# Another order for the last two token tiles, a shorter root, half-size own scores, and identity transposes in seven waits of PE

## What is computed

```python
x = x + _L0_xattn_ref(_layernorm(x), ctx_1024, ctx_1024, mask, gamma, beta)   # 64 queries on 1601 rows of context
x = x + _L0_attn_ref(_layernorm(x), W_qkv, W_out)                            # 64 tokens of a batch on each other
x = x + _L0_ffn_ref(_layernorm(x), router_w, expert_w1, expert_w2)           # top 2 of 8 experts, 512 -> 2048 -> 512

# in _L0_ffn_ref
scores = xf @ router_w.T
top_v, top_i = jax.lax.top_k(scores, 2)
routing_w = jax.nn.softmax(top_v, axis=-1)
for e in range(8):
    w_e = jnp.sum(jnp.where(top_i == e, routing_w, 0.0), axis=-1)
    h = jax.nn.gelu(xf @ expert_w1[e].T, approximate=False)
    out = out + h @ expert_w2[e].T * w_e[:, None]
```

## Time and profile before

| | us |
|---|---|
| median of 3 runs | 802.03 (801.93 to 803.76) |
| the profiled execution | 801.91, of it 800.3 between its first and its last instruction |
| PE busy | 740.5 of 800.3 |
| DVE, ACT, POOL busy | 447.5, 304.8, 148.5 |
| streaming stage, full turns (r = 3 to 7) | about 37 each |
| first expert chunk begins on PE | 382.36 |

### The profile page before, as it was taken

The page is one execution under the profiler, slowest core; times in us unless marked ns, Lnnn a source line. Parts: engine busy times, 40 slices in busy tenths (PEclk is TensorE's granted clock), DMA queues, the critical chain, the costliest instruction groups (busy, mean ns, idle before and its releaser), DMA issues.

```text
span 800.3 us, 12058 instructions
## 1 busy us (share of the span) xinstructions
PE 740.5 (93%) x4626; PEld 552.3 (69%) x4626; DVE 447.5 (56%) x1052; ACT 304.8 (38%) x508; POOL 148.5 (19%) x160
## 2 busy tenths in 40 slices
PE   5999899999999999862999899999999999999992
PEld 3453345364545453442999899999999998888882
DVE  4153467676868646755456544555556655566520
ACT  2031112122221211221555354556565565656620
POOL 2133030412213010104201021111210212120201
PEclk9999999999999999985899999999999999999997
DMA  9999999999999999211254455564755757674402
GB/s 340 401 421 383 421 384 384 418 379 423 381 421 367 421 412 400 120 52 35 88 163 183 119 176 186 141 208 161 209 189 170 208 205 205 215 235 167 122 1 27
DMA packets 35133, 198.85 MB, mean 248 GB/s; under 512 B 4540, under 2 KB 4924, under 8 KB 14080
## 3 DMA queue, kind: packets, MB, share of 16 engines
q1 hardware_dynamic: 29680, 187.81, 61.8%
q0 software_dynamic: 4672, 9.11, 6.1%
q10 hardware_dynamic: 720, 1.10, 0.4%
HBM read 188.16 MB, written 9.85 MB: 247 GB/s over the span
## 4 chain that ended last, share of the span: by engine, by line
PE 77%; DVE 8%; DMA 7%; issue 3%; SPq 2%; ACT 1%; POOL 1%; POOLq 0%; DVEq 0%; ACTq 0%
PE ps L756 8%; PE ps L985 8%; PE ps L797 8%; PE ps L987 8%; PE ps L986 8%; PE ps L1007 4%; PE ps L1008 4%; PE ps L1009 4%; PE ps L1014 4%; PE ps L1015 4%; PE ps L1016 4%; DMA arena<-in_w_out 3%; DMA arena<-in_ctx_turned 3%; PE ps L812 3%; PE ps L827 3%
## 5 line engine op out<-in xcount | busy, mean ns | idle before, releaser
L459 POOL TENSOR_TENSOR small<-small 128x1 f32<-128x1 f32 x64 | 20.9, 327 | 618.3 <-DVE yb_space L1510 198.0
L987 PE MATMUL ps<-xT,low_a 128*128 128x288 f32 (+5 forms) x384 | 111.1, 289 | 0.0
L1482 DVE TENSOR_TENSOR h_ring<-hid,h_ring 128x288 fp32r<-128x288 f32 (+5 forms) x128 | 55.6, 435 | 96.4 <-ACT h_ring L1173 93.4
L1168 ACT ACTIVATE hid<-ps 128x288 f32<-128x288 f32 (+5 forms) x128 | 50.6, 395 | 151.2 <-PE ps L987 148.7
L797 PE MATMUL ps<-arena 128*64 128x512 f32 (+1 forms) x416 | 94.5, 598 | 3.0 <-DMA arena<-in_ctx 1.8
L1371 DVE TENSOR_TENSOR low_a<-w_raw_a,high_b 128x2048 fp32r<-128x2048 f32 x32 | 73.2, 2291 | 37.7 <-ACT high_b L1108 36.4
L1061 ACT COPY arena<-ps 128x512 f32<-128x512 f32 (+2 forms) x93 | 43.8, 528 | 122.9 <-PE ps L731 66.7
L756 PE MATMUL ps<-arena 128*64 128x512 f32 x384 | 85.5, 596 | 0.9 <-DMA arena<-in_ctx_turned 0.7
L985 PE MATMUL ps<-xT,high_b 128*128 128x288 f32 (+5 forms) x256 | 74.9, 292 | 0.0
L987 PEld LDWEIGHTS ps<-xT,low_a 128*128 128x128 f32 x384 | 73.5, 191 | 0.0
L986 PE MATMUL ps<-xT,high_b 128*128 128x288 f32 (+5 forms) x256 | 73.4, 287 | 0.0
(11 more groups left out here) (192 smaller groups left out, 1615.7 us busy)
## 6 DMA issues: line engine op xcount, KB each, us to landing
arena<-in_ctx_turned SPq DMA_DIRECT2D x48, 1024.0 KB, 23.3
arena<-in_ctx SPq DMA_DIRECT2D x48, 1024.0 KB, 22.7
w_raw_a<-in_w SPq DMA_DIRECT2D x48, 1024.0 KB, 5.0
w_raw_b<-in_w SPq DMA_DIRECT2D x16, 1024.0 KB, 4.9
arena<-in_mask SPq DMA_DIRECT2D x8, 800.5 KB, 26.8
arena<-in_w_qkv SPq DMA_DIRECT2D x3, 1024.0 KB, 9.4
arena<-in_ctx SPq DMA_DIRECT2D x16, 130.0 KB
out<-res SPq DMA_DIRECT2D x8, 256.0 KB, 22.1
```

The costliest lines, as they stand in the source:

```text
L987: mm = pe.matmul(o, w_low[2 * f][:, cols], high[:, k, 0:w.width], start=False, stop=(k == KC - 1))
L1168: nc.scalar.activation(hid[:, c % 2, 0:w.width], bank(c % UP_BANKS)[:, 0:w.width], ACT.Gelu).then_inc(gelu_done, 1)
L1482: dve.tensor_tensor(h_ring[:, c % RING, 1, 0:w.width], hid[:, c % 2, 0:w.width], h_ring[:, c % RING, 0, 0:w.width].bitcast(F32), ALU.subtr ...
```

## The change

1. **The root** has 7 instructions in place of 9: the guess starts from another constant, a cubic step follows and one Newton step ends it. In `attended` the reciprocal of the row sum moves ahead of the wait for PE.
2. **`own_scores`** multiplies only the two diagonal blocks of 64 x 64 that are used, as 8 matmuls of 64 columns in place of 4 of 128.
3. **`route_first`** forms the difference of the two best scores earlier and signals it with a new semaphore, `ratio_set`, on which ACT's `gate_exp` waits in place of `picked`.
4. **`gates`** is new: five instructions of `route_second` (the token numbers and the two gates) become a function that is called ahead of it. `route_second` keeps four.
5. **The drain** has another order on PE, ACT and DVE, with `fill_order` to match.
6. **`keep_busy(n)`** on PE transposes the identity matrix n times into bank 0, and nobody reads that. It stands at seven places: 6, 16, 12 and 72 times in the drain, and 4 times behind each of the three `turn_x` of window 0.
7. **`gate`** of the last window's first piece waits for a new semaphore, `first_tile_done`, which PE sets at the last matmul of that piece.

```diff
-                    ("u", LAST), ("xr", LAST - 1), ("pt", LAST), ("logit", LAST - 1), ("out", LAST),
-                    ("rank", LAST - 1), ("xr", LAST), ("logit", LAST), ("rank", LAST)):
+                    ("u", LAST), ("pt", LAST), ("xr", LAST - 1), ("out", LAST), ("logit", LAST - 1),
+                    ("xr", LAST), ("logit", LAST), ("rank", LAST - 1), ("rank", LAST)):
...
+                pool.wait_ge(gates_ready, t + 1)
                 pool.wait_ge(pos_ready, t + 1)
...
             def own_scores(t):
                 wait_copied(pe, "g", t)
                 o = open_fill("s", t)
                 for k in range(KC):
-                    mm = pe.matmul(o[:, 0:P], gT[:, k, :], xnT[:, k, :], start=(k == 0), stop=(k == KC - 1))
+                    for b in range(2):
+                        q = slice(64 * b, 64 * b + 64)
+                        mm = pe.matmul(o[q, q], gT[:, k, q], xnT[:, k, q], start=(k == 0), stop=(k == KC - 1))
                 mm.then_inc(filled, 1)
...
+            def keep_busy(n):
+
+                for _ in range(n):
+                    pe.transpose(bank(0)[:, 0:P], ident, ident)
...
             turn_own_probs(LAST - 1)
+            keep_busy(6)
             turn_first(LAST)
             weigh(LAST - 1)
             keys(LAST)
             own_scores(LAST)
             values(LAST)
+            turn_own_probs(LAST)
             turn_second(LAST - 1)
-            turn_own_probs(LAST)
+            weigh(LAST)
             router(LAST - 1)
-            weigh(LAST)
-            ranks(LAST - 1)
+            keep_busy(16)
             turn_second(LAST)
             router(LAST)
+            ranks(LAST - 1)
+            keep_busy(12)
             ranks(LAST)
...
             pe.matmul(bank(6)[:, 0:EXPERTS], ones, cum[TILES], start=True, stop=True).then_inc(count_done, 1)
+
+            keep_busy(72)
...
+                        if final and w.kind == EXPERTS - 1 and t == 0:
+                            mm.then_inc(first_tile_done, 1)
...
                 turn_x(STATIC[0], t)
+                keep_busy(4)
...
             def gate_exp(t):
 
-                act.wait_ge(picked, t + 1)
+                act.wait_ge(ratio_set, t + 1)
...
             copy_probs(LAST)
-            copy_fill("xn", LAST - 1, xnT, shown=by_chunk)
             gate_exp(LAST - 2)
             for j in range(2):
                 split_high(STATIC[0], j)
+            copy_fill("xn", LAST - 1, xnT, shown=by_chunk)
...
             copy_fill("xr", LAST - 1, xrT, shown=by_chunk)
-            split_high(STATIC[0], 2)
+            for j in range(2, 4):
+                split_high(STATIC[0], j)
+            copy_fill("xr", LAST, xrT, shown=by_chunk)
             gate_exp(LAST - 1)
-            copy_fill("xr", LAST, xrT, shown=by_chunk)
-            split_high(STATIC[0], 3)
             gate_exp(LAST)
...
+            def rsqrt(variance):
+
+                own.then_next(dve.tensor_scalar(var, variance, EPS, ROOT_SCALE, ALU.add, ALU.mult))
+                own.then_next(dve.tensor_scalar(rstd.bitcast(I32), var.bitcast(I32), -0.5, GUESS, ALU.mult, ALU.add))
+                own.then_next(dve.scalar_tensor_tensor(out=half, in0=rstd, scalar=rstd, in1=var,
                                                        op0=ALU.mult, op1=ALU.mult))
-                own.then_next(dve.scalar_tensor_tensor(out=rstd, in0=half, scalar=1.5, in1=rstd,
+                own.then_next(dve.scalar_tensor_tensor(out=half, in0=half, scalar=-10.0 / 3.0, in1=half,
+                                                       op0=ALU.add, op1=ALU.mult))
+                own.then_next(dve.scalar_tensor_tensor(out=rstd, in0=half, scalar=5.0, in1=rstd,
+                                                       op0=ALU.add, op1=ALU.mult))
+                own.then_next(dve.scalar_tensor_tensor(out=half, in0=rstd, scalar=rstd, in1=var,
+                                                       op0=ALU.mult, op1=ALU.mult))
+                own.then_next(dve.scalar_tensor_tensor(out=rstd, in0=half, scalar=-64.0 / 3.0, in1=rstd,
                                                        op0=ALU.add, op1=ALU.mult))
...
             def attended(j):
 
+                dve.wait_ge(exp_done, j + 1)
+                own.then_next(dve.reciprocal(inv, rowsum[:, j % 2:j % 2 + 1]))
                 dve.wait_ge(pv_block, j * NBLK + NBLK)
                 moments(bank(NBLK - 1))
-                own.then_next(dve.reciprocal(inv, rowsum[:, j % 2:j % 2 + 1]))
...
+                    if n == 1:
+                        dve.tensor_tensor(ratio[par], best[:, 1:2], best[:, 0:1], ALU.subtract).then_inc(ratio_set, 1)
...
+            def gates(t):
 
                 par = t % 2
                 dve.wait_ge(places_free, t + 1)
+                own.then_next(dve.tensor_copy(meta_i[par][:, :, 1], token.to_broadcast([P, TOP_K])))
+                own.then_next(dve.tensor_scalar(token, token, float(P), None, ALU.add))
+                dve.wait_ge(ratio_ready, t + 1)
+                own.then_next(dve.tensor_scalar(low, ratio[par], 1.0, None, ALU.add))
+                own.then_next(dve.reciprocal(meta[par][:, 0, 0:1], low))
+                dve.tensor_tensor(meta[par][:, 1, 0:1], ratio[par], meta[par][:, 0, 0:1], ALU.mult).then_inc(gates_ready, 1)
...
             route_first(LAST - 2)
             for j in range(2):
                 split_low(STATIC[0], j)
+            gates(LAST - 2)
             route_second(LAST - 2)
...
             copy_pt(LAST)
+            second_norm(LAST)
             route_first(LAST - 1)
-            second_norm(LAST)
+            route_first(LAST)
+            gates(LAST - 1)
             route_second(LAST - 1)
-            route_first(LAST)
+            gates(LAST)
             route_second(LAST)
...
-                    dve.wait_ge(down_done, w.at(PER_CHUNK, FC))
+                    if w.kind == EXPERTS - 1 and t == 0:
+                        dve.wait_ge(first_tile_done, 1)
+                    else:
+                        dve.wait_ge(down_done, w.at(PER_CHUNK, FC))
```

More of the change, by code:

```diff
@@ L50 @@
 HUGE = 3.0e38
-GUESS = float(0x5F3759DF)
-NEWTON = 3
+GUESS = float(0x5F3759DF - 2 ** 31)
+ROOT_SCALE = (1024.0 / 27.0) ** 2
 C_ID, C_TRI, C_ONE, C_ME, C_SPARE, C_EXP = 0, P, 2 * P, 3 * P, 3 * P + 1, 3 * P + 2
@@ L408, in build @@
         xn2_ready = sem("xn2_ready")
-        picked, ratio_ready = sem("picked"), sem("ratio_ready")
+        picked, ratio_set, ratio_ready = sem("picked"), sem("ratio_set"), sem("ratio_ready")
+        gates_ready = sem("gates_ready")
         pos_ready = sem("pos_ready")
@@ L425, in build @@
         h_high_ready, h_ready = sem("h_high_ready"), sem("h_ready")
-        down_done = sem("down_done")
+        down_done, first_tile_done = sem("down_done"), sem("first_tile_done")
         yT_by_act, yT_by_dve = sem("yT_by_act"), sem("yT_by_dve")
@@ L1220, in _ @@
             own = Steps(dve, v_own)
-            def rsqrt_start(v, variance):
-                own.then_next(dve.tensor_scalar(v, variance, EPS, None, ALU.add))
-                own.then_next(dve.tensor_scalar(rstd.bitcast(I32), v.bitcast(I32), -0.5, GUESS, ALU.mult, ALU.add))
-                own.then_next(dve.tensor_scalar(v, v, -0.5, None, ALU.mult))
-            def rsqrt_step(v):
-                own.then_next(dve.scalar_tensor_tensor(out=half, in0=rstd, scalar=rstd, in1=v,
-                                                       op0=ALU.mult, op1=ALU.mult))
-                own.then_next(dve.scalar_tensor_tensor(out=rstd, in0=half, scalar=1.5, in1=rstd,
+            def rsqrt(variance):
+                own.then_next(dve.tensor_scalar(var, variance, EPS, ROOT_SCALE, ALU.add, ALU.mult))
+                own.then_next(dve.tensor_scalar(rstd.bitcast(I32), var.bitcast(I32), -0.5, GUESS, ALU.mult, ALU.add))
+                own.then_next(dve.scalar_tensor_tensor(out=half, in0=rstd, scalar=rstd, in1=var,
+                                                       op0=ALU.mult, op1=ALU.mult))
+                own.then_next(dve.scalar_tensor_tensor(out=half, in0=half, scalar=-10.0 / 3.0, in1=half,
[5 more added lines that the diff above has]
+                own.then_next(dve.scalar_tensor_tensor(out=rstd, in0=half, scalar=-64.0 / 3.0, in1=rstd,
                                                        op0=ALU.add, op1=ALU.mult))
@@ L1244, in normalize @@
                 moments(src)
-                rsqrt_start(var, mv[:, 1:2])
-                for _ in range(NEWTON):
-                    rsqrt_step(var)
+                rsqrt(mv[:, 1:2])
                 return dve.tensor_scalar(dst, src, mv[:, 0:1], rstd, ALU.subtract, ALU.mult)
@@ L1278, in attended @@
             def attended(j):
+                dve.wait_ge(exp_done, j + 1)
+                own.then_next(dve.reciprocal(inv, rowsum[:, j % 2:j % 2 + 1]))
                 dve.wait_ge(pv_block, j * NBLK + NBLK)
                 moments(bank(NBLK - 1))
-                own.then_next(dve.reciprocal(inv, rowsum[:, j % 2:j % 2 + 1]))
```

(14 more changed lines are left out.)

4 lines of the change are left out of this document (2 added, 2 removed).

## The result

The changed kernel takes 795.99 us (median of 4 runs, 794.73 to 796.58) against 801.98 before: a ratio of 0.992, 95% interval 0.9905 to 0.9935. That is 6.0 us less. The forecast was 792.4 with a range from 788.5 to 797.5, so the direction was right and the time lies in the range, but 3.6 us of the expected gain of 9.5 are missing. Where rows of two kernels are compared, part of a difference can be this.

A forecast was written before the change was run, and what follows sets the result against it. PE and full transfers were taken to bound the stream, one chain the drain, PE the expert stage. Stream 1.8, sending 5.4, clock and turning 1.6, end 0.7 sum to 9.5: 801.9 to 792.4 us, range 788.5 to 797.5.

The forecast's parts named there:

- stream, to `turn_own_probs` of tile 5: Streaming stage: shorter own_scores on PE, limited by waits for ACT while POOL holds DVE's cast; 1.8 us gained.
- from there to the norm of tile 7: Drain: shorter roots, own_scores, earlier gate_exp and the new order bring tile 7's norm 6.9 us earlier.
- places of tile 6, less the stream's: Drain, DVE: both route_first, gates and route_second follow the norm, so tile 6's places come only 1.4 us earlier.
- first transfer of send(7), less the stream's: Drain, POOL: the 3.92 us wait for DVE vanishes, POOL's own chain replaces it; tile 7 sent 5.4 us earlier.
- clock in the expert stage: First expert chunks: transposes may keep PE's fast clock; bounds 0 and 2.7 us, middle 1.3 taken.
- end: Last window: DVE gets the first piece before the last piece's matmuls end, so POOL starts 0.7 us earlier.
- at most 0.5 us earlier: Stream, turn 6: POOL's mask instruction cannot start before its mask lands, at most 0.5 us earlier than before.
- from there its own pace counts: Drain: once tile 6's places are sent, POOL needs 4.0 us until it is free for tile 7.
- Casts not held and clock held: First rival: POOL does not hold DVE's casts, stream gives 3.3, clock 2.7; 12.4 us gained, 789.5; chance 0.19.
- transposes don't lift the clock: Second rival, drain: transposes leave PE at 1.2 GHz; 3.0 us gained, 798.9; chance 0.13.
- they are serialised: Slower rival, drain: each of the 72 transposes waits for the one before, 30 us in all; 814; chance 0.03.
- The change doesn't move the chain: Rival, drain: POOL or its transfers stay late, landings 2 us slower, 4 of 9.5 gone; 796.4; within forecast's range.

The follow-up runs named there:

- e7: The changed kernel without the portion of 72 transposes, the six other portions kept; 795.22 us.
- e1: The changed kernel, with DVE starting split_low of blocks 2 and 3 only after POOL's addition in front of send(7); 795.33 us.
- e3: As e1, and tile 6 is finished on DVE before route_first of tile 7, with fill_order to match; 790.2 us.
- e6: The changed kernel, with DVE starting split_low of blocks 2 and 3 only after POOL has issued both transfers of send(7); 793.99 us.
- e8: The changed kernel with tile 6 finished on DVE before route_first of tile 7, without the additional wait ahead of the splits; 791.55 us.
- e10: As e8, without the portion of 72 transposes; 791.57 us.
- e11: As e8, without the portions of 4 transposes behind turn_x; 791.27 us.
- e2: The changed kernel without any identity transposes (keep_busy called nowhere); 798.46 us.
- e9: The changed kernel with only the portions of 4 transposes behind turn_x, without those of 6, 16, 12 and 72; 796.18 us.
- e4: The kernel before with the half-size own_scores and the short root alone; 796.68 us.
- e5: The kernel before with the half-size own_scores alone, the root keeping its 9 instructions; 800.05 us.
- e12: The kernel before with the short root alone; 798.97 us.

## Why the prediction was right or wrong

| step, gain in us | forecast | in the profiled execution |
|---|---|---|
| stream, to `turn_own_probs` of tile 5 | 1.8 | 3.0 (300.53 to 297.54) |
| from there to the norm of tile 7 | 6.9 | 6.4 (353.77 to 344.38, less 3.0) |
| places of tile 6, less the stream's | 1.4 | 1.4 (359.70 to 355.26, less 3.0) |
| first transfer of send(7), less the stream's | 5.4 | 1.2 (367.95 to 363.79, less 3.0) |
| first chunk, stream and turning included | 7.5 | 3.9 (382.36 to 378.48) |
| clock in the expert stage | 1.3 | 2.6 (chunk to PE's end, 403.60 to 401.04) |
| end | 0.7 | 0.8 |
| sum | 9.5 | 7.2; 6.0 between the medians |

- **The stream was mis-sized in two terms that err in opposite ways.** The cast of `gates` was held up by POOL as taken: L1370 lasts 5.08 us in turn 5, up to the end of POOL's mask instruction (in turns 3 and 4 DVE came just ahead of that). But "at most 0.5 us earlier" for POOL's start was wrong: it starts at 249.17 in place of 250.98 in turn 6. Before, its wait there ended with DVE's L1270, 0.6 behind the mask; now it ends with the mask, which lands earlier with the turn. So PE waits for ACT only once, 0.60 in turn 5. On the other side `own_scores` gives 0.44 per turn, not 0.53 to 0.6: the records are that much shorter, but the distance to `values` goes from 1.00 (145.81 to 146.81) to 0.56 (182.09 to 182.65), and turn 4 takes 36.80 (149.39 to 186.19) in place of 37.28. The rest is turn 3, 2.2 us earlier, where the old wait of 1.19 is gone.

  The rows of DVE and then POOL in the changed kernel, for the earlier trace rows:

```profile
212.82 5.08 DVE L1370 CAST route<-route 128x2 int32<-128x2 f32 x1
```

```profile
249.17 5.63 POOL L601 TENSOR_SCALAR arena<-arena 128x1601 f32<-128x1601 int32 x1
```

  Whether POOL holds the cast is a race, which neither the forecast nor its first rival foresaw. In turn 4 the cast is due at 175.6 to 176.5 and POOL begins at 175.6 to 176.3. It was held in turns 5 and 6 in the changed kernel (5.08 and 4.38) and e7, in turns 4 to 6 in e1, e3, e6, e8, e10 and e11 (3.9 to 5.5), and in none of the three in e2 and e9. Tile 5's `turn_own_probs` comes at 297.54 to 298.72 where it was held and at 296.61 (e2) and 296.16 (e9) where it was not. So the stream gave 1.8 to 3.0 us when held and 3.9 to 4.4 when not, against 1.8 and 3.3 in the prediction. Where the cast slips ahead, the last multiplication of `gates` is held in its place, but not as long: in turn 6 of e9 (L1371, 249.91, 4.11 us) until 254.02, 1.5 us ahead of the end of POOL's instruction. Turn 5 of e9:

```profile
212.35 0.16 DVE L1366 CAST route<-route 128x2 int32<-128x2 f32 x1
```

- **The drain to the norm** was right in sum, and the places of tile 6 too.
- **The step that failed is "from there its own pace counts", POOL's 4.0 us from tile 6 to tile 7.** From the first addition to the end of the last it was to take 4.0 and 0.2, and takes 8.4 (355.26 to 363.64). The 4.0 were read where DVE was doing small things. I moved POOL's chain by 5 us and didn't ask what DVE does at its new time: DVE's splits come behind the count, and moved forward with it into POOL's chain. Additions held for 1.15 and 2.06 us are 3.2 of it; e1, e6 and e3 show this. Another 0.7 is the landing of tile 6's records, 1.91 behind the issue in place of 1.22, and 0.33 a later issue behind the addition (355.45 to 355.93, before 359.89 to 360.04). The last is in every kernel with the additional wait on `gates_ready` and in none of before, e4, e5 and e12, which lack it; that this wait is its cause was not tested.
- **The clock came out at the upper bound by another way than argued.** I gave the gain to the 72. They end 7 us ahead of the rows, and the clock is down by then; the fours in the waits between the pieces bring it back (e2, e7, e9). The turning, in which I saw 0.3 of gain, costs 0.6: rows to first chunk is 4.91 us against 4.30 before, since four transposes at 1.2 GHz stand ahead of each next piece; without the fours it is 4.29 (e2).
- **The rivals.** Casts not held and clock held: neither is so in the changed kernel's profiled execution, and the first is so in e2 and e9. That transposes don't lift the clock is refuted by e9 and by the 72 themselves (0.50 from 358 to 360, 1.00 from 362 to 364), that they are serialised by 9.89 us for 72. "The change doesn't move the chain" was the nearest: 4 of 9.5 us gone between POOL and its transfers was its price, and at the first transfer of send(7) 4.2 were gone (5.4 forecast, 1.2 measured); its mechanism (slower landings) is 0.7 of that.
- **That the time lies in the range is in part luck.** At POOL 4.2 us were lost and in the turning 0.9, and stream and clock gave 1.2 and 1.3 more than summed.

## What to carry to other kernels

When a chain moves, look at what the other engines do at its new place, above all those that have held each other up elsewhere, as POOL and DVE did in the earlier trace rows; durations read at the old place hold only there. Here the remedy was to let the first of two sends go earlier, which a look at POOL's chain alone suggests, and it gave as much again as most of the change. Short work that keeps PE busy right ahead of a dense stage paid (the fours, 2.3 us), the same work separated from it by 7 us of rest did not (the 72). And a row's start in one execution moved by up to 2.6 us here with nothing changed ahead of it, so count from a common point, and read gains of a microsecond from the medians. The next stop is in the open already: from 436.03 PE stands still for 3.25 us in the changed kernel and waits for DVE, which comes from `count_more`, as it did before from 442.34; nothing was tried on it.

## What the runs showed of the hardware

- A DVE instruction with two inputs from SBUF held up both POOL's one-element additions (1.34 and 2.25 us in place of 0.19) and POOL's issuing of indirect transfers (2.76 and 1.87 in place of 0.98 and 0.96). The Trainium skill (SBUF — State Buffer, section SBUF: two separate sides) names the shared pair of ports an exclusive lock between a DVE instruction with two inputs from SBUF and a GpSimd one that reads SBUF, and (DMA: Bandwidth & Descriptors, section SWDGE vs HWDGE vs iDMA) says that GpSimd's descriptors are written into the memory from which DVE locks it out. The trace agrees with the first. For the issuing it shows that an instruction with two inputs holds it up too; whether it is the writing of the descriptors that is held was not tested.
- The other way round, POOL's mask instruction (5.63 us) held DVE's cast of two elements for up to 5.49 us (e7, turn 5; 0.16 unheld). Which of them started first decided it: a cast that began 0.03 us ahead of POOL's instruction took 0.16 us (212.35 against 212.38, e9), one that began 0.18 behind took 5.48 (175.80 against 175.62, e3).
- Transposes alone raised the clock: 4.92 us of them in 5.00, then 1.00 (e7). The Trainium skill (TensorE: Matmul & The Clock Gate, section Part 4: PE-mode transpose) says that they don't count as busy in the same way; this case speaks against it, with the 72 too: 0.50 from 358 to 360, 1.00 from 362 to 364, and nothing else on PE.
- The records of tile 6 landed 1.91, 1.93 and 1.54 us behind their issue in the changed kernel, e1 and e6, and 1.21 or 1.22 in all others. In these three alone a transfer of instructions on queue q8 falls into the same 3 us. The queues of the changed kernel from 357 to 360.2 (packets, MB, share):

```profile
q0 software_dynamic: 64, 0.02, 4.4%
q8 instruction: 1, 0.02, 2.7%
```

  In the other kernels the second line is missing in that stretch; in before and e5 there is one of 0.01 MB on q14, and the records still landed after 1.22. That one delays the other is likely from this, and was not tested.
